# Four normalisations of a pair moved from VectorE to ScalarE in a two-block transformer kernel

## The reference

```python
def _layernorm(x, axis=-1, eps=1e-05):
    m = jnp.mean(x, axis=axis, keepdims=True)
    v = jnp.var(x, axis=axis, keepdims=True)
    return (x - m) / jnp.sqrt(v + eps)
...
h = _layernorm(x, axis=-1) * (1 + ca) + sa          # norm1
x = x + ga * _L0_attn_ref(h, ...)                   # one head, softmax over 256 keys
h = _layernorm(x, axis=-1) * (1 + cb) + sb          # norm2
x = x + gb * _L0_ffn_ref(h, ...)                    # silu(gate) * up, all products quantised to FP4 by blocks of 16
...
h = _layernorm(x, axis=-1) * (1 + ca) + sa          # norm3
x = x + ga * _L1_attn_ref(h, ...)                   # 16 heads, causal
h = _layernorm(x, axis=-1) * (1 + cb) + sb          # norm4
x = x + gb * _L1_ffn_ref(h, ...)                    # 4 live experts of 704, the top 2 of them weighted
```

## Time and profile before

| | |
|---|---|
| median of three runs | 1906.71 us |
| profiled execution | 1907.06 us |
| its span, first to last instruction | 1905.3 us |
| TensorE busy | 1699.7 us, 89% |
| weight loads (beside the matmuls) | 1317.1 us, 69% |
| VectorE busy | 1678.0 us, 88% |
| ScalarE busy | 716.5 us, 38% |
| GpSimd busy | 68.9 us, 4% |

### The profile page before, as it was taken

How to read it: one execution, slowest core, us unless ns; L and a number is a source line. 1 busy time by engine, 2 the same in 40 slices (tenths; PEclk the granted TensorE clock), 3 DMA queues, 4 the chain that set the end, 5 groups by cost and what they waited for, 6 DMA issues and landing times.

```text
span 1905.3 us, 37018 instructions
## 1 busy us (share of the span) xinstructions
PE 1699.7 (89%) x12297; PEld 1317.1 (69%) x12297; DVE 1678.0 (88%) x3791; ACT 716.5 (38%) x1447; POOL 68.9 (4%) x78
## 2 busy tenths in 40 slices
PE   2347799999999999999999999999999999999998
PEld 1234567776776767677686767777676777768787
DVE  5578799989899998989989998999989899997775
ACT  0122435262533426253432526243352525334332
POOL 0000000000000000000000000000000000000000
PEclk7686899999999999999999999999999999999999
DMA  4020302003030301203030110303021030303000
GB/s 142 25 76 28 109 5 89 28 20 98 5 107 10 104 14 27 86 15 97 10 105 13 50 63 18 99 5 106 12 63 51 18 99 6 100 10 91 12 13 8
DMA packets 130106, 97.25 MB, mean 51 GB/s; under 512 B 28000, under 2 KB 124512, under 8 KB 125824
## 3 DMA queue, kind: packets, MB, share of 16 engines
q1 hardware_dynamic: 121536, 91.74, 16.4%
q10 hardware_dynamic: 8448, 4.20, 0.7%
HBM read 56.48 MB, written 29.98 MB: 45 GB/s over the span
## 4 chain that ended last, share of the span: by engine, by line
PE 47%; DVE 37%; issue 9%; ACT 4%; SPq 1%; DVEq 1%; DMA 1%; POOL 0%; ACTq 0%; POOLq 0%
DVE mneg L1099 9%; PE y_ps L1476 9%; PE bank L1469 5%; PE bank L1471 5%; PE bank L1470 5%; DVE h L1196 4%; PE bank L1220 4%; DVE tt L1188 3%; PE bank L1436 3%; ACT arena L770 2%; DVE xh L967 2%; PE bank L1343 2%; DVE arena L1107 2%; PE bank L1373 2%; PE bank L1420 2%
## 5 line engine op out<-in xcount | busy, mean ns | idle before, releaser
L813 ACT ACTIVATE tt<-bank 128x512 f32<-128x512 f32 x352 | 212.4, 603 | 665.8 <-PE bank L1471 523.9
L1476 PEld LDWEIGHTS y_ps<-wd,h 128*128 128x128 f32 (+1 forms) x3072 | 379.1, 192 | 70.7 <-issue 19.1
L1476 PE MATMUL y_ps<-wd,h 128*128 128x128 f32 (+1 forms) x3072 | 415.4, 282 | 14.1 <-DVE h L1196 14.1
L1196 DVE TENSOR_TENSOR h<-tt,bank 128x512 f32<-128x512 f32 x352 | 236.0, 682 | 23.6 <-PE bank L1471 7.1
L1188 DVE SCALAR_TENSOR_TENSOR tt<-tt,bank 128x512 f32<-128x512 f32 x352 | 237.2, 682 | 21.4 <-ACT tt L813 14.7
L1099 DVE TENSOR_REDUCE mneg<-bank 128x2 f32<-128x512 f32 (+1 forms) x384 | 236.0, 680 | 3.9 <-issue 2.4
L770 ACT ACTIVATE arena<-bank 128x512 f32<-128x512 f32 x384 | 196.5, 612 | 34.8 <-PE bank L1417 20.7
L1469 PE MATMUL bank<-h_hi,wg_hi 128*128 128x512 f32 x352 | 164.2, 466 | 10.3 <-DVE h_lo L1163 3.8
L1469 PE MATMUL bank<-h_hi,wu_hi 128*128 128x512 f32 x352 | 163.1, 463 | 8.4 <-DVE mneg L1099 8.3
L1107 DVE TENSOR_TENSOR arena<-arena,keep_k 128x1024 f32<-128x1024 f32 (+1 forms) x96 | 149.0, 1577 | 20.4 <-ACT arena L770 18.8
L1471 PE MATMUL bank<-h_lo,wg_hi 128*128 128x512 f32 x352 | 140.5, 399 | 0.0
(11 more groups left out here) (183 smaller groups left out, 2647.0 us busy)
## 6 DMA issues: line engine op xcount, KB each, us to landing
q_stack<-q_rows SPq DMA_DIRECT2D x16, 1024.0 KB, 4.8
k_stack<-k_rows SPq DMA_DIRECT2D x16, 1024.0 KB, 8.0
q_rows<-qk_halves SPq DMA_DIRECT2D x48, 256.0 KB, 2.8
k_rows<-qk_halves SPq DMA_DIRECT2D x48, 256.0 KB, 2.9
rows<-mod_rows SPq DMA_DIRECT2D x48, 128.0 KB, 3.0
rows<-mod_rows SPq DMA_DIRECT2D x16, 384.0 KB, 3.5
x_in<-in_L_attn_X SPq DMA_DIRECT2D x16, 256.0 KB, 2.8
vals<-arena SPq DMA_DIRECT2D x128, 32.0 KB, 5.2
```

Of the source, the lines that this page charges most:

```text
L813: send(a(tt[:, ch % 2, :], ps.bank(f"eg{ch}")[:], ACT.Tanh, scale=0.5), tanh_ready)
L1196: frees(v.tensor_tensor(h32[:, ch % 3], tt[:, ch % 2, :], ps.bank(f"eu{ch}")[:], ALU.mult), f"eu{ch}")
L1476: ins = mm(y_ps[:, P * t:P * (t + 1)], h32[rows_, ch % 3, P * t:P * (t + 1)], wd[rows_, ch, :], start=first and t == 0, stop=last_ and t = ...
```

## The change

The four norm steps leave VectorE's list and enter ScalarE's. ScalarE computes Identity(scale * x + bias) for each tile, with scale = rstd and bias = -mean * rstd, both one value per token. For this VectorE negates the means in stats (one instruction of 128x4 more), and GpSimd multiplies the negated means with rstd behind each power; between its two instructions it waits for its own semaphore. The signal rstd is now sent by the second of them.

```diff
             def root(it, n, var, rooted, rstd, k):
                 pool.wait_ge(var.sem, var.at(it, k))
-                send(g.tensor_tensor(n.rstd[:], n.ve[:], mhalf[:], ALU.pow), rstd)
+                send(g.tensor_tensor(n.rstd[:], n.ve[:], mhalf[:], ALU.pow), rooted)
+                pool.wait_ge(rooted.sem, rooted.at(it, k))
+                send(g.tensor_tensor(n.shift[:], n.mv[:, :, 0], n.rstd[:], ALU.mult), rstd)
...
+            def normalise(it, n, k, src, dst, rstd, done):
+                act.wait_ge(rstd.sem, rstd.at(it, k))
+                for t in range(TILES):
+                    last = a(dst[:, t, :], src[:, t, :], ACT.Identity, scale=n.rstd[:, t:t + 1], bias=n.shift[:, t:t + 1])
+                send(last, done)
+
+            def norm1(it):
+                normalise(it, n1, 1, x_in, xh1, rstd1_ready, xh1_ready)
...
                 step(last)
+                v.tensor_scalar(n.mv[:, :, 0], n.mv[:, :, 0], -1.0, None, ALU.mult)
                 send(v.tensor_scalar(n.ve[:], n.mv[:, :, 1], EPS, None, ALU.add), var)
-
-            def normalise(it, n, k, src, dst, rstd, done):
-                own(it, rstd, k)
-                for t in range(TILES):
-                    last = v.tensor_scalar(dst[:, t, :], src[:, t, :], n.mv[:, t, 0:1], n.rstd[:, t:t + 1], ALU.subtract, ALU.mult)
-                send(last, done)
...
 def sp_order(do):
 
-    do(1, "stack_v"), do(0, "load4"), do(1, "stack_max"), do(1, "load3"), do(1, "turn_att"), do(3, "load2"), do(4, "load1")
-    do(2, "store_q"), do(2, "store_k"), do(2, "stack")
+    do(1, "stack_max"), do(1, "stack_v"), do(0, "load4"), do(1, "turn_att"), do(3, "load2"), do(4, "load1"), do(2, "store_q")
+    do(2, "store_k"), do(2, "load3"), do(2, "stack")
```

More of the change, by code:

```diff
@@ L114, in act_order @@
-    do(0, "gate", 13), do(1, "turn_att"), do(3, "scores0", 0), do(0, "gate", 14), do(3, "scores0", 1), do(3, "probs0", 0)
-    do(3, "probs0", 1), do(0, "gate", 15), do(2, "turn3"), do(0, "gate", 16), do(2, "query1"), do(0, "gate", 17), do(2, "key1")
-    do(1, "turn4"), do(0, "gate", 18), do(1, "logits"), do(2, "value1"), do(0, "gate", 19), do(0, "gate", 20), do(1, "halves4")
-    do(0, "gate", 21), do(1, "gate", 0), do(1, "gate", 1), do(1, "gate", 2), do(3, "turn2"), do(1, "gate", 3), do(3, "gate0", 0)
@@ new lines, in act_order @@
+    do(0, "gate", 8), do(1, "carry"), do(2, "gate0", 3), do(0, "gate", 9), do(3, "key0"), do(0, "gate", 10), do(1, "rows", 0)
+    do(1, "rows", 1), do(0, "gate", 11), do(1, "rows", 2), do(3, "scores0", 0), do(1, "weigh", 0), do(1, "rows", 3)
+    do(1, "weigh", 1), do(1, "rows", 4), do(1, "rows", 5), do(0, "gate", 12), do(2, "turn_h", 0), do(1, "weigh", 2)
+    do(1, "weigh", 3), do(2, "turn_h", 1), do(2, "turn_h", 2), do(0, "gate", 13), do(2, "turn_h", 3), do(1, "turn_att")
+    do(3, "scores0", 1), do(0, "gate", 14), do(3, "probs0", 0), do(3, "probs0", 1), do(2, "norm3"), do(0, "gate", 15)
@@ new lines, in act_order @@
+    do(2, "turn3"), do(1, "norm4"), do(0, "gate", 16), do(2, "query1"), do(3, "norm2"), do(0, "gate", 17), do(2, "key1")
+    do(1, "turn4"), do(0, "gate", 18), do(1, "logits"), do(0, "gate", 19), do(1, "halves4"), do(0, "gate", 20), do(0, "gate", 21)
+    do(1, "gate", 0), do(2, "value1"), do(1, "gate", 1), do(3, "turn2"), do(1, "gate", 2), do(3, "gate0", 0), do(3, "gate0", 1)
+    do(1, "gate", 3), do(1, "gate", 4), do(1, "gate", 5), do(1, "gate", 6), do(0, "finish"), do(4, "norm1"), do(4, "turn1")
@@ new lines, in act_order @@
+    do(3, "gate0", 2), do(2, "turn_max"), do(4, "query0"), do(1, "gate", 7)
+def dve_order(do):
+    do(0, "swish", 7), do(0, "begin"), do(0, "times", 7), do(0, "mix", 0), do(0, "swish", 8), do(2, "quantise_h", 0, 2)
+    do(0, "times", 8), do(2, "gate0", 3), do(0, "swish", 9), do(2, "up0", 2), do(0, "swish", 10), do(2, "up0", 3)
+    do(0, "times", 9), do(2, "quantise_h", 1, 0), do(1, "cover", 0), do(0, "times", 10), do(1, "cover", 1), do(0, "swish", 11)
+    do(3, "scores0", 0), do(1, "cover", 2), do(2, "quantise_h", 1, 1), do(0, "times", 11), do(2, "quantise_h", 1, 2)
+    do(1, "cover", 3), do(1, "cover", 4), do(1, "cover", 5), do(1, "turn_out", 0), do(0, "swish", 12), do(1, "turn_out", 1)
+    do(3, "scores0", 1), do(1, "turn_out", 2), do(1, "turn_out", 3), do(0, "swish", 13), do(0, "mix", 1), do(3, "value0")
+    do(2, "down0"), do(0, "times", 12), do(2, "stats3"), do(0, "times", 13), do(0, "swish", 14), do(1, "add3"), do(0, "times", 14)
+    do(1, "stats4"), do(0, "swish", 15), do(3, "out0"), do(3, "stats2"), do(0, "times", 15), do(0, "swish", 16), do(2, "query1")
+    do(3, "modulate2"), do(0, "swish", 17), do(0, "times", 16), do(2, "key1"), do(3, "quantise_x", 0), do(0, "swish", 18)
+    do(1, "logits"), do(0, "times", 17), do(1, "route"), do(0, "times", 18), do(0, "mix", 2), do(3, "quantise_x", 1)
+    do(0, "swish", 19), do(0, "swish", 20), do(0, "times", 19), do(0, "times", 20), do(0, "swish", 21), do(1, "halves4")
+    do(0, "times", 21), do(3, "quantise_x", 2), do(1, "swish", 0), do(0, "finish"), do(1, "times", 0), do(4, "stats1")
+    do(1, "swish", 1), do(3, "gate0", 0), do(1, "swish", 2), do(1, "times", 1), do(3, "up0", 0), do(3, "gate0", 1)
+    do(1, "times", 2), do(3, "up0", 1), do(1, "swish", 3), do(3, "quantise_h", 0, 0), do(1, "swish", 4), do(2, "maxima", 0)
+    do(1, "times", 3), do(2, "maxima", 1), do(1, "times", 4), do(1, "swish", 5), do(1, "times", 5), do(2, "maxima", 2)
+    do(1, "swish", 6), do(2, "maxima", 3), do(2, "maxima", 4), do(2, "maxima", 5), do(3, "quantise_h", 0, 1), do(1, "times", 6)
+    do(2, "turn_max"), do(3, "gate0", 2)
@@ L1205, in finish @@
                 send(v.tensor_tensor(mixed[:], res[:], mixed[:], ALU.add), out_ready)
-            turns(dve, dve_order, dict(norm1=norm1, value0=value0, scores0=scores0, out0=out0, norm2=norm2, modulate2=modulate2,
-                            quantise_x=quantise_x, gate0=gate0, up0=up0, quantise_h=quantise_h, down0=down0, norm3=norm3,
+            turns(dve, dve_order, dict(value0=value0, scores0=scores0, out0=out0, modulate2=modulate2,
+                            quantise_x=quantise_x, gate0=gate0, up0=up0, quantise_h=quantise_h, down0=down0,
                             query1=query1, key1=key1, turn_max=turn_max, maxima=maxima, cover=cover, turn_out=turn_out, add3=add3,
-                            norm4=norm4, logits=logits, route=route, halves4=halves4, begin=begin, stats1=stats1, stats2=stats2, stats3=stats3,
+                            logits=logits, route=route, halves4=halves4, begin=begin, stats1=stats1, stats2=stats2, stats3=stats3,
                             stats4=stats4, swish=swish, times=times, mix=mix,
```

103 lines of the change are left out of this document (41 added, 62 removed), and 46 rows, old and new, of the table USES.

## The result

The changed kernel takes 1914.51 us (median of 22 runs, 1906.40 to 1931.33) against 1905.77 (22 runs of before beside them): a ratio of 1.0052, 95% interval 1.0032 to 1.0071. It is slower by 0.5%; forecast was 1872, and the range ended at 1903. The profiled execution took 1922.66 us, with a span of 1920.9.

What follows compares the result with a forecast made beforehand. VectorE (105.3 us of a 109.5 us turn) and TensorE (103.4) were both taken as almost full. A 106.7 us turn saves 2.75, times 14 is -38.5, plus 4 at the start: 1872 us, range 1846 to 1903.

Steps and rivals of the forecast that it cites:

- the wait of modulate2: On VectorE, modulate2 must wait for ScalarE's normalised xh2: a new wait of 1.1 us a turn (0.2 to 2.9).
- scores0's: VectorE's 1.7 us wait for the first attention's scores, moved between two covers; half counted as gone, -0.85 us a turn.
- product for the rows: TensorE's first product on the rows of maxima, after reordered SP DMAs; expected not to wait for a DMA, cost 0.
- The start: Before 200 us, six powers each awaited by the whole chain; each norm 0.65 us longer, together +4 us.
- The prediction's own signs of being wrong: A turn under 105.5 or over 108 us, or a wait not named there costing over 1 us a turn.
- The sum: Per turn, VectorE's side gave 105.95 us and TensorE's 107.5; the middle, 106.7, was taken, 2.75 less than before.
- the old excess of 4.1: The turn's time beyond the fuller engine's work, for handing banks over; added to TensorE's 103.4 it gave 107.5 us.
- Times 14: From 200 to 1732 us, 14 equal turns each save 2.75 us, together -38.5 us.
- TensorE takes it back: Seven banks tie TensorE and VectorE, so VectorE's relief becomes waiting; gain 0 to 1.5 us a turn, 1888 to 1911; chance 0.19.
- Norm2 holds up ScalarE: norm2 waits for GpSimd with ScalarE's gates, key1 and turn4 queued behind; slower, 1912 to 1926 us; chance 0.12.
- VectorE alone: VectorE is the only bound, so all its relief arrives: -4.35 us a turn, 1850 us; chance 0.12 (below 1858).
- the port: GpSimd's second operation and VectorE's add3 wait on their shared port; at most 1.0 us a turn, 1887 us; chance 0.04.

Runs made afterwards that it cites:

- hyb: The kernel before, its orders kept, with the four normalisations moved to ScalarE and GpSimd's product added; 1928.8 us, ratio 1.0124.
- rotv: The new orders with rot's ends of the turns, but the four normalisations left on VectorE; 1933.1 us, ratio 1.0132 against before.
- dve_rot: a_pad with VectorE's end of a turn alone moved back, from behind gate0 2 to behind maxima 4; 1889.1 us, ratio 0.9904 against before.
- rot: The kernel after with the end of a turn moved back on TensorE, VectorE and ScalarE, each engine's sequence unchanged; 1884.0 us, ratio 0.9879 against before.
- unr: The kernel after without a loop, its 11 turns written out; 1889.5 us, ratio 0.9886 against before.
- unrb: The kernel before without a loop; 1886.5 us, ratio 0.9910.
- a_pad: The kernel after with 320 already satisfied waits ahead of TensorE's first wait, shifting its loop in the code; 1911.0 us, ratio 1.0031 against before.
- b_pad: The kernel before with 244 already satisfied waits ahead of TensorE's first wait, putting its loop where after has it; 1949.7 us, ratio 1.0240.
- unrm: The kernel after without a loop and with VectorE's modulate2 three steps later, behind key1; 1872.7 us, ratio 0.9831 against before.
- pe_rot: The kernel after with TensorE's end of a turn alone moved back by its last 9 steps; 1902.6 us, ratio 0.9990 against before.
- b_exp: The kernel before with VectorE's end of a turn alone moved on, to in front of swish 7; 1933.6 us, ratio 1.0142.
- hyb2: hyb with norm3 and norm2 on ScalarE each one step later, behind gate 15 and gate 17; 1897.6 us, ratio 0.9952 against before.

## Why the prediction was wrong

**The prices were right, or nearly.** A norm on ScalarE lasts 1.65 us (four of 0.48), forecast 1.5; GpSimd's product 0.20; VectorE busy 98.1 (98.5 to 99), ScalarE 50.6 (50), GpSimd 5.4 (4.8), the wait of modulate2 1.1 (1.1), scores0's gone, no product for the rows waits for a DMA. The start is later by 4.1 us as forecast (+4), but for another reason: in hyb, with the same normalisations, the first power of rstd_b starts at 212.8, before's 213.5, and in rotv, without them, at 216.2. It is the new orders that start later, and that the sizes agree is luck. The prediction's own signs of being wrong came: a turn over 108, and waits of 1.9 and 1.6 us that it does not name.

**The turn was right for a kernel that was not built.** The sum gave 106.7. dve_rot, which is after with VectorE's jump elsewhere and TensorE's loop at another place in its code, has 106.6 to 106.7 in turns at the full clock, and before 109.5. There is luck in this too. The 106.7 is the middle of two sums, and neither has a term for the new orders themselves, which cost 1.1 us a turn (before to rotv), nor for the loop, which costs before 1.8 and dve_rot 1.2; the move gave up to 3.5 (rotv to rot).

**The step that failed** is "The sum", in what it left out: "109.45 - 3.75 - 0.85 + 1.1" and "if the old excess of 4.1 stays" take the end of a turn and the clock for fixed. The new orders moved both. Both were put at nothing without a reason. Of the 110.88 us of a middle turn, by an estimate from differences between the profiled executions:

- 105.4 is the turn without a loop at the full clock (unr);
- 1.2 a loop with VectorE's jump behind maxima 4 (dve_rot, 106.6; unrb says that before pays 1.8 of this kind);
- 1.3 VectorE's jump, and the fetch that starts with it, in front of swish 7 (a_pad, 109.4 less 1.55 for one slow stretch, 107.85, against 106.6);
- 0.5 the 9 packets of TensorE's code (turns with one slow stretch each: after 109.85, a_pad 109.2 to 109.6);
- 2.4 the clock: 14 slow stretches in nine turns, 1.55 us each; before had 2, 0.35.

The sum is 110.8 of 110.88. The 1.3, the 0.5 and the clock's 2.4 - 0.35 are what the forecast lacks, 3.85 us a turn: they turn a gain of 2.9 (109.5 to 106.6) into a loss of 1. The first two are shown by moving the jump and the loop. The clock's part is read from one execution, the one with the lowest clock; that some of it goes with the jump shows in dve_rot, that not all does in unr, and why it fell more often is open.

**Times 14 was too many.** I took every turn from 200 to 1732 us as full. rot gains 21.8 us against before in the nine middle turns (2.4 each), but only 1.7 in the three ahead of them, 2.2 in the three behind, and it loses 3.1 at the start and 4.5 at the end. Forecast were -25 for the nine, -8 for the three ahead, -5.5 for the last (two full turns), +4 at the start and nothing at the end. That is why even rot, with the forecast's turn wherever the clock is full, takes 1884 and not 1872: of the 16 us that its profile lies over the forecast 3 are in the nine turns, 6.5 in front of them, 3.3 behind them and 4.5 at the end, less 0.9 at the start. The loss at the end is there with the normalisations on VectorE as well (rotv, 80.6 us behind the last power against 76.2) and in the old orders too (hyb, 82.5); its cause wasn't tried.

**The rivals.** "TensorE takes it back" described the waits of after (TensorE 51% of the chain, VectorE's waits 9.0 for 4.1), but its mechanism, the seven banks, is not what cost the time: with the same banks and sequences rot gives 30 us back. "Norm2 holds up ScalarE" does not occur in after, where modulate2 waits 1.1 us; it is what makes hyb slow, with 4.1 us of waits a turn and 1929 us for a priced 1912 to 1926. But there the waits are swish's for the tanh behind norm3 and norm2, and not modulate2's, by which the prediction meant to tell (3.6 us). "VectorE alone" did not come: the fastest kernel here takes 1871 us at the least, against the rival's 1850. Its turn, 109.45 - 4.35 = 105.1, is nearly reached only without a loop and at the full clock (105.4). On the port, GpSimd's product beside add3, in order of time:

```profile
1087.75 0.69 DVE L1132 TENSOR_TENSOR xh<-arena,rows 128x512 f32<-128x512 f32 x1
1087.77 0.72 POOL L639 TENSOR_TENSOR shift_a<-mv_a,rstd_a 128x4 f32<-128x4 f32 x1
...
1092.54 0.20 POOL L639 TENSOR_TENSOR shift_b<-mv_b,rstd_b 128x4 f32<-128x4 f32 x1
```

The same kind of product takes 0.72 us beside a VectorE operation with two operands in SBUF, and ends with it, and 0.20 at 1092.54, where VectorE runs an operation with a bank as operand. Of the 64 products in the profile 14 last 0.68 to 0.73, all of them beside L1132, and the others 0.20. It is GpSimd that waits, so the 14 us of that rival did not come. The Trainium skill ("SBUF — State Buffer", section "SBUF: two separate sides") has just this pair of operations exclude each other for a whole instruction; the trace agrees.

## What to carry to other kernels

A written order also says where each engine's loop ends, and that is a cost of its own: 21 us in nine turns here for the same work, 9 of them by the clock. Before pricing a new order, look up in the profile what each engine does at the jump, how long it idles there with no releaser, and how many packets of code each queue fetches in a turn, and when they start; a few steps moved across the end of the turn, or some padding ahead of the loop, set most of it right here, and writing the loop out is the test of what it costs (1.8 us a turn even where the profile showed 0.2). Then compare turns at the same granted clock: idle gaps of 1 to 2 us on TensorE can cost twice, once as gaps and once as slow products behind them (half of after's did). Last, put a step that waits for another engine behind the step that somebody else needs, not in front of it.

## What the runs showed of the hardware

- TensorE's code comes in packets of 16 KB. With a loop of 6.6 blocks that begins at 12.93, 12.98 or 14.04 blocks the turns had no packets; with one that begins at 13.41 there were 9 a turn, in both kernels tried (after, b_pad). In line there are about 6 a turn, and no cost of them shows (unr, unrm).
- At VectorE's jump an 8 KB packet of code is fetched in every turn, and the next instruction starts 1.9 to 2.1 us after the packet's start. With short steps in front of the jump VectorE idles 1.9 to 3.3 us (after, a_pad, pe_rot, b_exp), with the maxima's reductions there 0.2 to 0.8 (before, dve_rot, rot, hyb2).
- A stretch of 3.4 us at 1.2 GHz costs a turn 1.6 us in unr, by turns with the same instructions, and 0.5 to 1.8 in others.
- An ACTIVATE of 128x128 from SBUF with a scale and a bias per row takes 0.48 us, and four in a row 1.65 (after).
- A GpSimd product of 128x4 takes 0.20 us, and 0.72 beside a VectorE product of 128x512 with both operands in SBUF, ending with it (after).
